# Routing and experts in one block, interleaved one-hot rows, and LayerNorm aggregates moved in the encoder steps

## What is computed

```
Xh = rfft(chunks of 64 rows)                       # 33 frequencies, 16 chunks a sequence
low 4 frequencies : block-causal attention, 16 heads (4 key heads), real and imaginary part
high 29           : causal depthwise conv (7 taps), GELU, 128x128 product, gate, + X_high
x1 = layernorm(x + irfft(low and high joined))
dist = distance of each row of x1 to 8 centroids;  w, sel = top_k(dist, 2);  w = softmax(w)
out  = sum over the two experts e: w_e * ((silu(x1 Wg[e] + bg[e]) * (x1 W1[e] + b1[e])) W2[e] + b2[e])
y = layernorm(x1 + out)
```

## Time and profile before

| | us |
|---|---|
| median of 3 runs | 645.86 (643.2 to 646.05) |
| the profiled execution | 644.24 |
| its span, first to last instruction | 642.4 |

### The profile page before, as it was taken

How to read it: one execution, slowest core, us unless ns; L and a number is a source line. 1 busy time by engine, 2 the same in 40 slices (tenths; PEclk the granted TensorE clock), 3 DMA queues, 4 the chain that set the end, 5 groups by cost and what they waited for, 6 DMA issues and landing times.

```text
span 642.4 us, 13675 instructions
## 1 busy us (share of the span) xinstructions
PE 527.2 (82%) x3845; PEld 494.8 (77%) x3845; DVE 507.2 (79%) x1312; ACT 356.1 (55%) x751; POOL 321.7 (50%) x482
## 2 busy tenths in 40 slices
PE   2788998999996531024999999999999999999971
PEld 2677887888885330023999999999999999999971
DVE  3669988989986547893477788989898989899983
ACT  3476877987886131021555555575656565656651
POOL 0223654655563222095544444456777776544644
PEclk9879999999999755556899999999999999999995
DMA  9141315504520210100000000011111111000000
GB/s 228 38 120 56 117 39 153 143 27 135 153 57 9 65 35 5 10 6 14 23 20 18 20 19 18 19 28 35 35 31 36 36 35 34 27 23 11 33 26 33
DMA packets 49866, 31.68 MB, mean 49 GB/s; under 512 B 14112, under 2 KB 47472, under 8 KB 49808
## 3 DMA queue, kind: packets, MB, share of 16 engines
q1 hardware_dynamic: 44864, 21.39, 12.6%
q0 software_dynamic: 4224, 8.75, 4.9%
q10 hardware_dynamic: 720, 0.82, 0.4%
HBM read 22.25 MB, written 8.69 MB: 48 GB/s over the span
## 4 chain that ended last, share of the span: by engine, by line
PE 46%; DVE 3%; issue 2%; POOL 1%; DMA 0%; ACT 0%; DVEq 0%; POOLq 0%; SPq 0%
PE ps L1181 22%; PE ps L1199 12%; PE ps L1189 7%; PE ps L1200 4%; DVE xs L1370 1%; PE ps L1213 1%; DVE h L1353 1%; DMA xs<-rows_dram,idx 0%; POOL out_dram L1154 0%; ACT hh L1274 0%; POOL xs L1150 0%; DVE bn L1302 0%; DVE y L1328 0%; DVE mv L1310 0%; DVE yb L1326 0%
## 5 line engine op out<-in xcount | busy, mean ns | idle before, releaser
L1181 PE MATMUL ps<-wts,xh 128*128 x624 | 167.9, 333 | 0.4 <-issue 0.4
L1199 PE MATMUL ps<-wts,hh 114*128 (+1 forms) x468 | 119.7, 341 | 3.7 <-DVE xs L1370 3.1
L1370 DVE SCALAR_TENSOR_TENSOR xs<-ps,xs 128x128 f32 x312 | 108.3, 347 | 17.9 <-DVE xs L1370 11.7
L1163 POOL TENSOR_TENSOR xl<-xT,xh 127x128 fp32r<-127x128 f32 x156 | 68.5, 459 | 106.9 <-ACT xh L1255 106.9
L1181 PEld LDWEIGHTS ps<-wts,xh 128*128 128x128 f32 x624 | 113.3, 193 | 0.8 <-issue 0.7
L1200 PE MATMUL ps<-wts,hl 114*128 (+1 forms) x468 | 104.9, 224 | 0.0
L1181 PE MATMUL ps<-wts,xl 128*128 x312 | 100.7, 323 | 0.0
L1266 ACT ACTIVATE sg<-ps 128x684 f32<-128x684 f32 x78 | 57.9, 742 | 74.2 <-PE ps L1181 74.2
L1274 ACT ACTIVATE hh<-ps 114x768 fp32r<-114x768 f32 x78 | 63.4, 812 | 57.2 <-PE ps L1189 57.2
L1199 PEld LDWEIGHTS ps<-wts,hh 114*128 114x128 f32 (+1 forms) x468 | 89.0, 190 | 7.6 <-issue 7.6
L1200 PEld LDWEIGHTS ps<-wts,hl 114*128 114x128 f32 (+1 forms) x468 | 90.4, 193 | 0.0
(11 more groups left out here) (225 smaller groups left out, 992.4 us busy)
## 6 DMA issues: line engine op xcount, KB each, us to landing
xt<-_attn_hidden_states_dram SPq DMA_DIRECT2D x8, 512.0 KB, 5.0
xres<-_attn_hidden_states_dram SPq DMA_DIRECT2D x8, 512.0 KB, 4.5
rows_dram<-x1s SPq DMA_DIRECT2D x8, 512.0 KB, 3.5
st<-in_L_ffn_W_dram SPq DMA_DIRECT2D x16, 171.0 KB
st<-in_L_ffn_Wg_dram SPq DMA_DIRECT2D x8, 171.0 KB
stl<-in_L_ffn_Wg_dram SPq DMA_DIRECT2D x8, 171.0 KB
stl<-in_L_ffn_W_dram SPq DMA_DIRECT2D x8, 171.0 KB
xs<-rows_dram,idx POOLq DMA_INDIRECT x64, 2.6
```

The costliest lines, as they stand in the source:

```text
L1163: v.tensor_tensor(xl[0:D - 1, i % 2, u, :], xT[0:D - 1, bass.ds(off[u], P)], xh[0:D - 1, i % 2, u, :].bitcast(F32), ALU.subtract).then_inc ...
L1181: mm = pe.matmul(ps[:, 2 * w + u, 0:HF], a[:, t % 2, u, :], wflat[:, bass.ds(w1[u] + (b + w * HF), HF)], start=(k == 0), stop=(k == 2))
L1199: pe.matmul(ps[:, 6 + u, 0:2 * D], hh[0:n, t % 2, u, k, :], w2flat[0:n, bass.ds(at, 2 * D)], start=(k == 0), stop=False)
L1370: v.scalar_tensor_tensor(out=row, in0=ps[:, 6 + u, k * D:(k + 1) * D], scalar=xsflat[:, bass.ds(off[2 + u], 1)], in1=row, op0=ALU.mult, op ...
```

## The change

- Phase 1: VectorE's aggregates, seeds and copy `lg` of step t - 1 (now `finish`, `logits`) come in step t, behind the `XL` copies and ahead of the convolution. The first and the last step differ only in which semaphores and copies they have.
- `route` and `experts` share one block. `xs`, the four gather semaphores and a new one, `placed`, are made ahead of both. `idx` is written once the bias pieces and the row weights have landed, and raises `placed`; GpSimd then issues the first four gathers. VectorE's four memsets of `experts` stay where they were in its stream; TensorE, ScalarE and GpSimd wait for them only before the first use.
- One-hot rows: laid out as groups of four tiles with the four tiles innermost; all operands are bf16; VectorE makes the third product too; GpSimd only makes `io4` (each number 0 to 127 four times) and `iob`, ahead of its bias work and behind `s_oh`. TensorE reads with a step of four elements.
- `up` takes the products of `xh` first and those of `xl` third, and waits for each half by itself.
- TensorE makes two spare products of 512 columns behind the inverse; nothing reads them.

```diff
+            def logits(t):
+                dve.wait_ge(s["r_done"], t - 1)
+                v.tensor_copy(lg[:, bass.ds((t - 2) * TB, TB), :], ps[:, 7, :]...[:, :, 0:E]).then_inc(s["lg_ev"], 1)
+
+            def finish(t, first, T):
+                dve.wait_ge(s["bn_done"], TB * t)
+                if not first:
+                    dve.wait_ge(s["sq_done"], t - 1)
+                dve.sem_inc(s["bn_seen"], 1)
+                for j in range(TB):
+                    v.bn_aggr(mv[:, j, :], bn[:, j, :]).then_inc(s["mv_done"], 1)
...
+                if T:
+                    logits(t)
@@ step, behind the XL copies
+                if T:
+                    early = isinstance(t, int) and t == 2
+                    finish(t - 1, early, not early)
                 if X:
                     conv(t, 0, not Y, range(KS))
@@ step, behind bn_stats
-                    (the same aggregates and seeds, and at the step's end the copy lg)
@@ route, vector
-            v.tensor_copy(iob[:, :], con("iota"))
...
+            v.tensor_copy(hib[:, :], hif[:, :])
+            link(v.scalar_tensor_tensor(out=lob[:, :], in0=hif[:, :], scalar=-float(P), in1=pos[:, :], ...))
...
+            dve.wait_ge(s_io, 2)
             for c in range(4):
-                part = slice(c * NT // 4, (c + 1) * NT // 4)
-                shape = (P, NT // 4, P)
-                v.tensor_tensor(hieq[:, part, :], iob[:, 0:NT].unsqueeze(1).broadcast_to((P, NT // 4, NT)),
-                                hif[:, part].unsqueeze(2).broadcast_to((P, NT // 4, NT)), ALU.is_equal).then_inc(s_hi, 1)
-                v.tensor_tensor(lohot[:, part, :], iob[:, :].unsqueeze(1).broadcast_to(shape),
-                                lof[:, part].unsqueeze(2).broadcast_to(shape), ALU.is_equal).then_inc(s_hot, 1)
+                part = slice(c * NQ // 4, (c + 1) * NQ // 4)
+                def over_m(a, m):
+                    return a.rearrange("p (c j) -> p c j", j=TQ)[:, part, :].unsqueeze(2).broadcast_to((P, NQ // 4, m, TQ))
+                def over_c(m):
+                    return io4[:, 0:m, :].unsqueeze(1).broadcast_to((P, NQ // 4, m, TQ))
+                v.tensor_tensor(hieq[:, part, :, :], over_c(NT), over_m(hib[:, :], NT), ALU.is_equal).then_inc(s_hi, 1)
+                v.tensor_tensor(lohot[:, part, :, :], over_c(P), over_m(lob[:, :], P), ALU.is_equal).then_inc(s_hot, 1)
+                dve.wait_ge(s_hi, c + 1)
+                v.tensor_tensor(hihot[:, part, 1, :, :], hieq[:, part, :, :], over_m(iob[:, :], NT), ALU.mult).then_inc(s_hit, 1)
...
+            dve.wait_ge(s_bout, 64)
+            dve.wait_ge(s_wd, 16 * B)
+            v.scalar_tensor_tensor(out=idx[:, :], ...).then_inc(placed, 1)
@@ route, gpsimd
+            pool.wait_ge(s_oh, 1)
+            v.tensor_copy(iob[:, :], con("iota")[:, 0:NT]).then_inc(s_io, 1)
+            v.tensor_copy(io4[:, :, :], con("iota").unsqueeze(2).broadcast_to((P, P, TQ))).then_inc(s_io, 1)
...
-            (the four products hihot, and the wait for the bias pieces)
+            v.memset(xs[:, 0, RD:ROW], 0.0)
+            pool.wait_ge(placed, 1)
+            for k in range(GATS):
+                v.indirect_dma_start(xs[:, k, 0:RD], None, g["rows_dram"], bass.IndirectOffsetOnAxis(idx[:, k:k + 1], 0)).then_inc(gat[k], 16)
@@ route, tensor
-                    pe.matmul(ps[:, 0, 0:2 * NT], lohot[:, t, :], hihot[:, t, :, :]..., start=False, stop=False)
+                    pe.matmul(ps[:, 0, 0:2 * NT], lohot[:, t // TQ, :, t % TQ], hihot[:, t // TQ, :, :, t % TQ]..., start=False, stop=False)
...
+            for _ in range(2):
+                pe.matmul(ps[:, 6, :], ident, cr[:, 0:512], start=True, stop=True)
@@ experts, gpsimd
-            for t in range(-GAHEAD, LAST + 1):
+            for t in range(-1, LAST + 1):
...
+                    if i == 0:
+                        pool.wait_ge(s["prep"], 4)
@@ experts, up
-                    for k, (a, b) in enumerate(((xh, 0), (xl, 0), (xh, 2 * HF))):
+                    if w == 0:
+                        pe.wait_ge(s["xh_done"], 2 * t + u + 1)
+                    for k, (a, b) in enumerate(((xh, 0), (xh, 2 * HF), (xl, 0))):
+                        if w == 0 and k == 2:
+                            pe.wait_ge(s["xl_done"], 2 * t + u + 1)
@@ experts, tensor
-                    pe.wait_ge(s["xl_done"], 2 * (t + 1))
```

More of the change, by code:

```diff
@@ L32 @@
 W2 = 4 * HF
+GATS = 4
 F32 = mybir.dt.float32
@@ L785, in phase2, with sem @@
 def phase2(nc, g):
-    route(nc, g)
-    experts(nc, g)
+    with ExitStack() as ctx:
+        xs = ctx.enter_context(nc.sbuf_tensor("xs", [P, NT, ROW], F32))
+        def sem(name):
+            return ctx.enter_context(nc.semaphore(name))
+        gat = tuple(sem("gat%d" % i) for i in range(GATS))
+        placed = sem("placed")
+        block = ctx.enter_context(nc.Block())
+        g = dict(g, xs=xs, gat=gat, placed=placed, sem=sem, block=block)
+        route(nc, g)
+        experts(nc, g)
 def top_two(nc, g, lo, hi, link):
@@ L820, in route @@
 def route(nc, g):
-    ps, cr, ident, c2, lg, sq, cn, rows_t, idx, steptab, wts = (g[k] for k in ("ps", "cr", "ident", "c2", "lg", "sq", "cn", "rows_t", "idx", "steptab", "wts"))
+    ps, cr, ident, c2, lg, sq, cn, rows_t, idx, steptab, wts, xs, gat, placed, block = (
+        g[k] for k in ("ps", "cr", "ident", "c2", "lg", "sq", "cn", "rows_t", "idx", "steptab", "wts", "xs", "gat", "placed", "block"))
     order = pair_order()
@@ L844, in route @@
         trimb = sb("trimb", [P, P], BF16)
-        iob = sb("iob", [P, P], BF16)
+        iob = sb("iob", [P, NT], BF16)
         zb = sb("zb", [P, P], BF16)
@@ L852, in route @@
         hif = sb("hif", [P, NT])
-        lof = sb("lof", [P, NT])
-        lohot = sb("lohot", [P, NT, P], BF16)
-        hieq = sb("hieq", [P, NT, NT], BF16)
-        hihot = sb("hihot", [P, NT, 2, NT], BF16)
+        TQ = 4
+        NQ = NT // TQ
+        lohot = sb("lohot", [P, NQ, P, TQ], BF16)
+        hieq = sb("hieq", [P, NQ, NT, TQ], BF16)
+        hihot = sb("hihot", [P, NQ, 2, NT, TQ], BF16)
+        io4 = sb("io4", [P, P, TQ], BF16)
+        lob = sb("lob", [P, NT], BF16)
+        hib = sb("hib", [P, NT], BF16)
         inv = sb("inv", [P, 2 * NT])
@@ L881, in route @@
                              "weights", "weights_out", "difference", "units", "table"))
-        block = ctx.enter_context(nc.Block())
         @block.vector
@@ L945, in _ @@
             link(v.tensor_copy(hif[:, :], hii[:, :]))
-            link(v.scalar_tensor_tensor(out=lof[:, :], in0=hif[:, :], scalar=-float(P), in1=pos[:, :], op0=ALU.mult, op1=ALU.add))
+            v.tensor_copy(hib[:, :], hif[:, :])
+            link(v.scalar_tensor_tensor(out=lob[:, :], in0=hif[:, :], scalar=-float(P), in1=pos[:, :], op0=ALU.mult, op1=ALU.add))
             dve.wait_ge(s_ex, 1)
@@ L1001, in _ @@
             link(v.tensor_copy(inv[:, :], ps[:, 0, 0:2 * NT]))
-            link(v.scalar_tensor_tensor(out=idx[:, :], in0=inv[:, NT:], scalar=float(P), in1=inv[:, 0:NT], op0=ALU.mult, op1=ALU.add))
+            dve.wait_ge(s_bout, 64)
+            dve.wait_ge(s_wd, 16 * B)
+            v.scalar_tensor_tensor(out=idx[:, :], in0=inv[:, NT:], scalar=float(P), in1=inv[:, 0:NT], op0=ALU.mult, op1=ALU.add).then_inc(placed, 1)
         @block.scalar
@@ L1035, in _ @@
                 pool.dma_start(wts[D - 1:D, :, 2 * k * HF:2 * (k + 1) * HF], parts[k:k + 1]).then_inc(s_bout, 16)
-            for c in range(4):
-                part = slice(c * NT // 4, (c + 1) * NT // 4)
-                pool.wait_ge(s_hi, c + 1)
-                v.tensor_tensor(hihot[:, part, 1, :], hieq[:, part, :], con("iota")[:, part].unsqueeze(2).broadcast_to((P, NT // 4, NT)),
-                                ALU.mult).then_inc(s_hit, 1)
-            pool.wait_ge(s_bout, 64)
+            v.memset(xs[:, 0, RD:ROW], 0.0)
+            pool.wait_ge(placed, 1)
+            for k in range(GATS):
+                v.indirect_dma_start(xs[:, k, 0:RD], None, g["rows_dram"], bass.IndirectOffsetOnAxis(idx[:, k:k + 1], 0)).then_inc(gat[k], 16)
         @block.tensor
@@ L1093, in experts @@
 def experts(nc, g):
-    ps, cr, ident, idx, steptab, rows, out, wts = (g[k] for k in ("ps", "cr", "ident", "idx", "steptab", "rows_dram", "out", "wts"))
+    ps, cr, ident, idx, steptab, rows, out, wts, xs, gat, placed, block = (
+        g[k] for k in ("ps", "cr", "ident", "idx", "steptab", "rows_dram", "out", "wts", "xs", "gat", "placed", "block"))
     out_rows = out.rearrange("b s d -> (b s) d")
     GAHEAD, TAHEAD = 4, 2
-    GATS = 4
     DONE = SETTLE + 3
```

56 lines of the change are left out of this document (23 added, 33 removed).

## The result

| | before | after |
|---|---|---|
| median, us | 644.61 (4 runs, 643.2 to 646.05) | 629.45 (4 runs, 628.64 to 630.71) |
| profiled execution | 644.24 | 628.64 |
| its span | 642.4 | 626.8 |

The ratio is 0.975 (0.9725 to 0.978). The forecast was 632.3 us, and 630.6 for a profiled execution; measured were 629.45 and 628.64. The span is 15.6 us shorter, where 13.6 was forecast. Of the 2.85 us between 632.3 and 629.45, 1.25 lie in the start of the sum: it began at the median of 645.86, and with a fourth run the kernel before has 644.61.

A forecast was written before the change was run, and what follows sets the result against it. TensorE's work bounds the experts' 78 iterations and stays, so time comes from the other three stages: -14.8 + 1.2 + 0 + 0 = -13.6 us, from 645.86 to 632.3 us; own range 629 to 636, wider range 625 to 641.

The forecast's parts named there:

- Part 1: Between `idx` and the first gather: the joined block, with GpSimd waiting on `placed` alone, gains 2.8 us.
- Part 2: Routing before the one-hot rows: GpSimd's bias work no longer collides with VectorE's instructions, 1.8 us gained; cast changes counted too.
- Part 6: The experts' 78 iterations: reordered products and four waits instead of one change nothing, 0 us.
- Part 3: One-hot rows and table up to `idx`: faster bf16 rows and an idle GpSimd; with part 1, first gather 14.8 us earlier.
- Part 5: Encoder steps 2 to 7: aggregates moved behind `XL` copies lengthen each step by 0.20 us, +1.2 us in all.
- Part 4: Experts' start: the first product still comes 6.2 us after the first gather, clock low again, gain 0.
- The wake-up: Ahead of the first gather: GpSimd's 0.28 us from the end of its wait to the gather stays.
- the bound of 2.5: Routing: `io4` on GpSimd takes at most 2.5 us, at the rate of its L1040, at least 0.
- TensorE's term: One-hot products in the routing: 0.104 us each despite stepped reads, as the array's pace at half clock; upper end twice that.
- the clock stays up: Rival at the experts' start: clock stays high through the gathers, 3.0 us less 0.3 gained, 629.6 us; chance 0.12.
- The term of 6 x 0.20: Encoder: six steps each grow by 0.20 us, growth 1.07 against slack 0.87, giving +1.2 us.
- the rival of costly waits: Experts' iterations: 234 added waits at 0.086 us each cost 20.1 us, 652.4 us, slower than before; chance 0.03.

The follow-up runs named there:

- e12: Kernel before with only the joined block and the first gathers waiting on `placed` alone; 641.8 us, ratio 0.9957.
- e9: Kernel after with GpSimd's bias work put back ahead of the two casts and their wait; 630.85 us (one execution).
- e5: Kernel after with one-hot groups of one tile instead of four; 639.61 us (one execution).
- e8: Kernel after with two unread GpSimd products of 1024 elements beside the one-hot rows and the table; 629.88 us (one execution).
- e3: Kernel before with two Newton refinements instead of three in the encoder steps; 640.54 us, ratio 0.9931.
- e6: Kernel after with one-hot groups of two tiles instead of four; 628.99 us (one execution).
- e4: Kernel after without TensorE's two spare products; 630.28 us, ratio 0.976.
- e11: Kernel after with groups of two tiles, four spare products instead of two, and one more behind each of the first three transposes; 627.29 us, ratio 0.9736.
- e1: Kernel after with phase 1 as before: aggregates, seeds and logits at the end of a step again; 630.51 us, ratio 0.9766.
- e10: Kernel after with five waits instead of one on each half of `xh`, 624 more in all; 632.15 us (one execution).
- e7: Kernel after with one-hot groups of sixteen tiles instead of four; 636.73 us (one execution).

## Why the prediction was right

The forecast and its range held, and so did the mechanisms of parts 1, 2 and 6. Part 3 held for VectorE, but two of its readings of the kernel before did not. In part 5 the growth was overstated, and the step did not grow. The 0.65 us of part 4 are chance, and so are the 1.25 us of the baseline.

- **Part 1, right.** 2.79 us measured against 2.8; e12 shows it alone. The wake-up came out at 0.27 us against 0.28.
- **Part 2, right.** -1.92 against -2.04. e9 brings 1.65 us of it back by the order on GpSimd alone, so the cause is shown. `io4` took 0.61 us, far below the bound of 2.5, and hid as foretold; the bound came from the 4.9 us of L1040, which is a mean of unlike instructions (part 3).
- **Part 3, right, by a sum in which two sizes were off a little.** A quarter took 2.34 us instead of 2.50, because the rows ran at 0.52 ns an element and not 0.56: 10.0 forecast, 9.43 measured. L912 was the right row to take the rate from, and e5 shows the other end of the range (4.47 against 4.48). The table took 1.43 us against 1.7, and e8 shows that GpSimd's work was what stretched it. The sentence that GpSimd paced a quarter of the old rows with 4.9 us is wrong: its first product took 13.89 us and the other three 1.90 each. VectorE's rows were done at 286.45, and the 7.4 us to 293.8 were GpSimd's four products one after another; on VectorE they cost 0.60 each. The forecast took only the end at 293.8 from that reading, so the sum did not suffer. TensorE's term was 0.104 us a product at a stepped read, "the array's own pace at half clock". The number nearly came out (2.04 us for the last 16, where 1.7 was forecast), but its reason failed: the clock was at 1.00 by then, and the stepped read alone kept a product at about 0.12. The 0.104 was no pace at half clock either. It is the mean of 64 products, of which those behind 293.7 ran at 1.00; 16 of that layout at 1.00 take 1.05 us (e3). With the reason wrong, the forecast could not see that groups of two are better by 0.96 us (e6).
- **Part 4, right but for 0.65 us that are not the change's.** The first product came 6.32 us after the gather, as forecast (6.2), at half clock, as forecast. The spare products took 1.94 us and not 3.4, because the clock was at 1.00 when they ran; so they ended at 284.8 instead of 286.6 and left 1.81 us idle. The 0.65 us come from the clock, which was back after 3.4 us of products instead of 5.9. It isn't the spare products' work, since e4 has it too (3.4 us, 12.31 in all), nor the new order of `up`, since e12, with the old one, takes 12.31. Nor does it need the change at all: e3 has the experts' start of the kernel before, word for word, and takes 12.18 us. Kernels with one and the same start took from 12.1 to 13.1 us, by where the clock's rise fell; what sets that moment stays open. So the 0.65 us are luck. The rival "the clock stays up" was wrong for the change, but e11 shows that it was a real one: 3.0 - 0.3 = 2.7 us below the kernel before by the forecast, 12.84 - 10.74 = 2.1 measured.
- **Part 5, mechanism right, size off.** The forecast set a growth of 1.07 us against a slack of 0.87, and so +0.20 a step. Measured against the end of `XF` (131.93 before, 132.69 after), `nmr` starts at +7.05 and +7.90: a growth of 0.85. Of the missing 0.22, 0.14 are in VectorE's instructions behind `XL`, which overlap it more (`lg` ends at 134.57 - 132.69 = 1.88, where 2.02 was forecast), and the rest on GpSimd. Then the slack took it as listed: the 0.61 ahead of `x1T` is used up and leaves 1.02 - 0.76 = 0.26, and the sum behind the second Exp starts at +17.12 instead of +17.14. (The 0.31 us there were no wait of VectorE in the kernel before, as the prediction calls them: it was at work, and the Exp was early by that much. As slack they count the same.) So the slack was 0.92 less 0.03 for the wake-up, against 0.85, where the forecast had 0.87 against 1.07, and the loop step didn't grow. The term of 6 x 0.20 should have been the 1.09 us by which the first interval grew, once, less small gains in the later ones: +0.27 in all. The difference between two sums of near equal size can't carry a sign: here both were within 0.2 us of each other, and e1 can't tell them apart by time.
- **Part 6, right.** -0.1 measured; e10 closes the rival of costly waits, the only one that would have made the kernel slower: at most 0.001 us each in the iterations, and at most 0.3 us in all at the start.

The expectation for e3 in its turn missed: only the last two steps were to gain, 2 to 3 us; the early steps gained 1.1 and the end 4.3.

## What to carry to other kernels

- Ask of a short instruction that takes five times too long what the neighbouring engine does in that moment. Here 1.65 us came from moving the neighbour behind a wait, with no work removed, and about 4 us of table work from giving GpSimd's products to VectorE. And look at each instruction of a run before you use its mean: 4.9 us was the mean of 13.89 and three of 1.90.
- Put a broadcast operand's repeat anywhere but innermost, and interleave as few elements as the fast rate of one engine needs, since TensorE, which reads them, can pay for a wider step: two were better than four, and sixteen lost 7.4 of the 10.4 us.
- When a wait on the bound engine can be removed by delaying another chain, add up both circles, and treat a difference smaller than the errors of the two sums as zero.
- Spare products kept the clock up into the dense work only when they filled every gap ahead of the dense work: two at its start were worth 0.12 us, less than the spread, and all gaps filled 1.45 us.

## What the runs showed of the hardware

- TensorE's reads of two-byte operands depend on the step. At a granted clock of 1.00, 16 products of 128 columns took 1.05 us with both operands without a gap (e3), 1.08 us at a step of 4 bytes and 2.04 us at 8 bytes; at 32 bytes each took 0.24 us, at 0.50. No run steps one operand alone. The pace at 8 bytes is the same at either clock: 48 products in 5.86 us, most of them at 0.50, and 16 in 2.04 at 1.00.
- The clock's rise is not at a fixed distance from the experts' first product: 5.9 us in the kernel before, 3.4 after and in e4, 3.2 in e6, 6.2 in e7. In e7 it stayed at 0.50 through all 15.5 us of the products at a step of 32 bytes, which follow one another without a gap. In the kernel after it fell at 290.3, behind three transposes with gaps of 1 to 1.8 us, as the dense products began. With a product of 512 or 256 columns behind each transpose it stayed (e11).
- GpSimd and VectorE wait for one another by whole instructions. VectorE's f32 instructions on SBUF, two-source and one-source ones, went from 0.22 to between 1.4 and 2.0 us beside a GpSimd instruction, and each ended 0.08 to 0.10 us behind it (L994 and L995 at 288.31 and 290.18 behind 288.21 and 290.08 in the kernel before, L834 in e9, L1023 and L1024 in e8). L996, which reads PSUM, kept its 0.30. The other way round, a GpSimd product of 1.9 us took 13.89 and 10.55 us beside VectorE's two-source one-hot rows, which kept their pace, and ended 1.8 to 1.9 us behind the last of them.
- `maskT` writes 512 two-byte elements at a wide step in 2.44 us, with GpSimd idle; a like instruction with a dense output (`we`, 512 elements of f32) takes 0.69. No run here took that apart.
- A wait on a semaphore that is already raised, or soon will be, costs TensorE's queue at most 0.001 us in the experts' iterations (e10).
